# Other places for a batch's products in an attention and MLP block of eight batches, and doubled products without reader in batches 0 and 1

## The reference

```python
mod = (_silu(c) @ wmod).reshape(8, 6, 1, 128)            # sa, ca, ga, sb, cb, gb
h = _layernorm(x) * (1 + ca) + sa
q, k, v = split(h @ w_qkv.T)                             # 16 heads of 8
s = q @ k.T * 8 ** -0.5
s = s - max(s)
p = where(s >= 0, 1 + s*(1 + s/2*(1 + s/3)), 1 / (1 - s*(1 - s/2*(1 - s/3))))
x = x + ga * ((p / sum(p)) @ v @ w_out.T + b_out)
h = _layernorm(x) * (1 + cb) + sb
h = s0 * concat(h, -h) @ W0; h = relu(h) * 2
h = s1 * h @ W1;             h = relu(h) * 2
x = x + gb * (s2 * h @ W2)
```

## Time and profile before

| | |
|---|---|
| median of 3 runs | 709.76 us |
| the profiled execution's own time | 708.76 us |
| its span, first to last instruction | 706.9 us |
| TensorE (PE) busy | 627.4 us, 3019 products |
| VectorE (DVE) busy | 646.2 us |
| ScalarE (ACT) busy | 598.8 us |
| GpSimd (POOL) busy | 599.0 us |
| mean granted TensorE clock | 0.97 of full |

### The profile page before, as it was taken

How to read it: one execution, slowest core, us unless ns; L and a number is a source line. 1 busy time by engine, 2 the same in 40 slices (tenths; PEclk the granted TensorE clock), 3 DMA queues, 4 the chain that set the end, 5 groups by cost and what they waited for, 6 DMA issues and landing times.

```text
span 706.9 us, 9679 instructions
## 1 busy us (share of the span) xinstructions
PE 627.4 (89%) x3019; PEld 244.5 (35%) x3019; DVE 646.2 (91%) x768; ACT 598.8 (85%) x606; POOL 599.0 (85%) x390
## 2 busy tenths in 40 slices
PE   7577787877789999899989999899989999997798
PEld 5222222223222344233423333233423343334266
DVE  6899988989999999999999999999999999998943
ACT  2647877978899999999999989999999989998932
POOL 7769777897989999899989999899989989798920
PEclk9579999999999999999999999999999999999999
DMA  7514112141124222141224122241125112101001
GB/s 206 160 46 165 48 51 61 54 149 32 55 58 144 81 58 73 48 159 32 57 76 168 50 58 75 60 167 41 40 61 172 53 54 72 54 10 27 17 12 30
DMA packets 37783, 53.61 MB, mean 76 GB/s; under 512 B 11308, under 2 KB 20804, under 8 KB 37732
## 3 DMA queue, kind: packets, MB, share of 16 engines
q1 hardware_dynamic: 36766, 51.81, 24.1%
q10 hardware_dynamic: 966, 1.19, 0.6%
HBM read 29.17 MB, written 18.36 MB: 67 GB/s over the span
## 4 chain that ended last, share of the span: by engine, by line
PE 56%; DVE 17%; ACT 12%; issue 11%; POOL 2%; SPq 1%; DMA 1%; ACTq 0%; DVEq 0%; POOLq 0%
PE MB L515 13%; PE OP L593 12%; PE Z L561 9%; PE SA L576 8%; DVE cub L966 8%; DVE mx L975 7%; ACT sq L720 5%; ACT prob L734 4%; PE MB L528 3%; PE MB L505 2%; PE MB L612 2%; PE MB L486 1%; PE OP L443 1%; DVE st L1012 1%; PE MB L493 1%
## 5 line engine op out<-in xcount | busy, mean ns | idle before, releaser
L1201 POOL TENSOR_TENSOR cub<-cub 128x2048 f32<-128x2048 f32 x127 | 456.8, 3602 | 48.4 <-DVE cub L966 48.1
L720 ACT ACTIVATE sq<-Z,shift 128x1024 f32<-128x1024 f32 x256 | 282.3, 1116 | 58.5 <-PE Z L561 56.8
L966 DVE SCALAR_TENSOR_TENSOR cub<-sq,Z 128x1024 f32<-128x1024 f32 x256 | 309.8, 1211 | 13.0 <-ACT sq L720 12.2
L975 DVE TENSOR_REDUCE mx<-SA 128x2 f32<-128x1024 f32 x248 | 301.9, 1217 | 15.6 <-PE SA L576 12.2
L734 ACT ACTIVATE prob<-cub 128x2048 f32<-128x2048 f32 x128 | 244.3, 1910 | 0.4 <-PE OP L593 0.4
L576 PE MATMUL SA<-KH,QL 64*128 64x512 f32 x496 | 121.1, 485 | 33.4 <-DVE mx L975 29.3
L561 PE MATMUL Z<-QH,KH 64*128 64x512 f32 x512 | 128.8, 499 | 17.7 <-DVE cub L966 16.5
L593 PE MATMUL OP<-prob,Vq 128*16 128x512 f32 x1024 | 136.6, 607 | 0.0
L561 PEld LDWEIGHTS Z<-QH,KH 64*128 64x128 f32 x512 | 48.4, 185 | 197.6 <-DVE cub L966 121.6
L515 PE MATMUL MB<-hid,W 128*128 128x512 f32 x192 | 108.0, 645 | 0.0
L576 PEld LDWEIGHTS SA<-KH,QL 64*128 64x128 f32 x496 | 47.4, 187 | 111.1 <-DVE mx L975 89.4
(11 more groups left out here) (205 smaller groups left out, 501.6 us busy)
## 6 DMA issues: line engine op xcount, KB each, us to landing
QL<-parts_q SPq DMA_DIRECT2D x62, 128.0 KB, 2.6
KH<-parts_k SPq DMA_DIRECT2D x62, 128.0 KB, 2.7
QH<-parts_q SPq DMA_DIRECT2D x62, 128.0 KB, 2.7
parts_q<-SQ SPq DMA_DIRECT2D x28, 256.0 KB, 2.5
parts_k<-SK SPq DMA_DIRECT2D x28, 256.0 KB, 2.7
QH<-mp SPq DMA_DIRECT2D x253, 2.0 KB
nd<-OT SPq DMA_DIRECT2D x124, 32.0 KB
out<-y SPq DMA_DIRECT2D x7, 256.0 KB, 2.8
```

What stands on the lines that cost most here:

```text
L720: nc.scalar.activation(sq[:, h, :], Z[:, h, :], ACT.Square, bias=shift[:, 0:1]).then_inc(s_sq, 1)
L966: nc.vector.scalar_tensor_tensor(cub[:, m % RING, h, :], sq[:, h, :], CUB_ADD, Z[:, h, :], ALU.add, ALU.mult).then_inc(s_cv, 1)
L975: nc.vector.tensor_reduce(to, unit_bank(m, u)[:, :, :], AX_X, ALU.max).then_inc(s_mx, 1)
L1201: nc.gpsimd.tensor_tensor(ff, ff, ff, ALU.mult).then_inc(s_fp, 1)
```

## The change

It gives new places to all products of batches 0 to 6 in `MAIN`, to l0 in batch 7, and to l1_3 of batch 6; it issues two products instead of one at each place of `FILL`, and takes other places for it; it moves xbg and wog; it turns the order of SyncE's queue in a step; it moves batch 6's x1n from VectorE to GpSimd, and changes the order behind the last step.

```diff
 MAIN = [
-    ("hT", 1, [(0, "c", 4)]), ("q", 1, [(0, "d", 4)]), ("k", 1, [(1, "d", 4)]),
-    ("l1_0", -2, [(2, "c", 1), (2, "d", 1), (3, "c", 1), (3, "d", 1)]),
-    ("l1_1", -2, [(4, "c", 1), (4, "d", 1), (5, "c", 1), (5, "d", 1)]),
-    ("l1_2", -2, [(6, "c", 1), (6, "d", 1), (7, "c", 1), (7, "d", 1)]),
+    ("l1_0", -2, [(0, "c", 1), (0, "d", 1), (1, "c", 1), (1, "d", 1)]),
+    ("hT", 1, [(2, "c", 4)]), ("q", 1, [(2, "d", 4)]), ("k", 1, [(3, "c", 4)]),
+    ("l1_1", -2, [(3, "d", 1), (4, "c", 1), (4, "d", 1), (5, "c", 1)]),
+    ("l1_2", -2, [(5, "d", 1), (6, "c", 1), (6, "d", 1), (7, "c", 1)]),
+    ("v", 1, [(7, "d", 4)]),
     ("x1", -1, [(8, "c", 2), (8, "d", 2)]),
     ("l1_3", -2, [(9, "c", 1), (9, "d", 1), (10, "c", 1), (10, "d", 1)]),
-    ("v", 1, [(11, "c", 4)]),
-    ("y", -2, [(11, "d", 1), (12, "c", 1), (12, "d", 1), (13, "c", 1)]), ("h2T", -1, [(13, "d", 4)]),
+    ("y", -2, [(11, "c", 1), (11, "d", 1), (12, "c", 1), (12, "d", 1)]), ("h2T", -1, [(13, "d", 4)]),
...
-    ("l0_0", -1, [(11, "c", 4)]), ("l0_1", -1, [(12, "c", 4)]), ("l0_2", -1, [(13, "c", 4)]), ("l0_3", -1, [(14, "c", 4)]),
+    ("l0_0", -1, [(12, "b", 4)]), ("l0_1", -1, [(13, "b", 4)]), ("l0_2", -1, [(14, "b", 4)]), ("l0_3", -1, [(15, "b", 4)]),
...
-    ("l1_2", -2, [(2, "c", 4)]), ("l1_3", -2, [(4, "b", 2), (4, "c", 2)]), ("y", -2, [(5, "c", 3), (5, "d", 1)]),
+    ("l1_3", -2, [(0, "b", 3), (0, "c", 1)]), ("l1_2", -2, [(2, "c", 4)]), ("y", -2, [(5, "c", 3), (5, "d", 1)]),
...
-FILL |= {(0, n): ("k", 2) for n in range(2, 12)} | {(0, n): ("v", 2) for n in range(12, 16)}
-FILL |= {(1, n): ("k", 3) for n in range(2, 8)} | {(1, n): ("x1", 1) for n in range(9, 12)} | {(1, 12): ("v", 3)}
+FILL = {(FIRST, n): ("v", 1) for n in range(13, 16)} | {(0, n): ("v", 1) for n in range(3)}
+FILL |= {(0, n): ("k", 2) for n in range(4, 8)} | {(0, n): ("v", 2) for n in range(8, 16)}
+FILL |= {(1, n): ("v", 2) for n in range(3)} | {(1, n): ("k", 3) for n in range(4, 8)}
+FILL |= {(1, n): ("x1", 1) for n in range(9, 14)}
...
-MAIN_AT = {"xbg": 6, "wog": 5, "den_sq": 6, "den_inv": 6, "att": 7, "st2": 9, "mv2": 10, "rs2": 11, "x1n": 11,
+MAIN_AT = {"xbg": 1, "wog": 2, "den_sq": 6, "den_inv": 6, "att": 7, "st2": 9, "mv2": 10, "rs2": 11, "x1n": 11,
...
-AT[B] = MAIN_AT | {"w2g": 0, "wog": 1, "xbg": 1}
+AT[B] = MAIN_AT | {"xbg": 0, "wog": 0, "w2g": 1}
...
-                    product(B, "l1_3", B - 2): (SA[:, 0, :], product(B - 1, "l1_0", B - 2)),
+                    product(B, "l1_3", B - 2): (Z[:, 1, 0:S], None),
...
                     pe.wait_ge(s_wts, 1)
-                    nc.tensor.matmul(MB[:, :], ident[:, :], W1f[:, n % KC, :], start=True, stop=True)
+                    for kc in (n % KC, (n + 1) % KC):
+                        nc.tensor.matmul(MB[:, :], ident[:, :], W1f[:, kc, :], start=True, stop=True)
```

107 lines of the change are left out of this document (50 added, 57 removed).

## The result

The changed kernel took 722.74 us in the median of 4 runs (722.69 to 723.08); the kernel before, run beside it, 709.23 (706.82 to 710.2). The ratio is 1.019, 95% interval 1.017 to 1.021: slower by 13.5 us, where a time of 715, some 5 us slower, was forecast; 722.74 lies above the range of 711 to 719 and the wider one of 708 to 721. The profiled execution took 722.73 us, with a span of 720.9 against 706.9.

The account below looks back on a forecast made before the run. VectorE's work sets the floor, 4.54 us a step; in batches 0 and 1 the SA loop, 4.62, is just over it. Terms 0.4 - 0.9 + 4.0 + 4.2 - 1.0 - 1.3 = +5.4 gave 714.2, as median 715, range 711 to 719.

Parts of the forecast that it names:

- The start: Steps ahead of batch 0, where three places are doubled too: +0.4 us, bounds 0 and 2.6.
- Batch 0, steps 0 to 4: No `with_v` yet, so VectorE's floor holds; with hT, q and k some 0.9 more: 24.0 against 24.9 us, -0.9.
- Batch 0, steps 5 to 15: Eleven doubled places in the loop between SA products, 5.48 each, 0.2 for v: 60.5 against 56.5 us, +4.0.
- Batch 1: Twelve doubled places, 65.8 us, with hT, k, x1 and statistics priced by step: 86.0 against 81.8, +4.2.
- The clock: TensorE's clock taken as full from batch 0 on; by the skill's idle rule three falls would stay, 5 us more.
- Batches 2 to 6: Moved products: -1.6 from ScalarE's full stretch, +1.1 from four late steps, +0.3 KH wait: -0.2 us a batch.
- Batch 7 to step 15: x1n leaving VectorE gives -2.3, l0 at place b costs +3.5: step 15 starts 1.1 us later.
- Behind it: Behind batch 7's last steps, l1_3 fills PE's wait and identity products precede the pick: -2.4 of 42.2 us.
- A: Rival: the second product is free in batches 0 and 1, about 4.7 us a step, total about 699; chance 0.08.
- B: Rival: the clock stays low over the start of batch 0, +5 us, total 720; chance 0.12.
- C: Rival: the middle gives all it can, -1.5 us a batch in batches 2 to 6, total about 708.7; chance 0.12.
- D: Rival: the KH read is late behind the writes, 1 us more in five batches, +5, total 720; chance 0.13.

Follow-up runs that it names:

- e2: The changed kernel with l0 of batch 7 put back at place c of steps 11 to 14; 719.40 us.
- e3: The changed kernel with the second product without reader moved behind the second SA product of its step, in 22 of 27 places; 711.72 us.
- e5: The changed kernel with product v back in step 11 at place c, and y a half step later; 726.62 us.
- e6: The changed kernel with l0 of batch 7 at its old places and x1n of batch 6 on VectorE again; 722.53 us.
- e1_single: The changed kernel with one product without reader, not two, at each place of FILL; 716.30 us.
- e4_before_doubled: The kernel before with two products at each of its own places of FILL, nothing else changed; 721.95 us.
- e17_x1n_gpsimd: The same kernel as e16, with batch 6's x1n on GpSimd; 693.96 us.
- e14: The kernel before with the new end, products without reader at place d (none in step 11), new places for l1_0, hT, q, k, and early writes of parts; 694.93 us.
- e16: The same kernel as e14, with the products without reader doubled ahead of batch 0 and in its steps 0 to 2; 694.69 us.
- e11_sp_order: The kernel before with SyncE's order of the change alone; 716.51 us.
- e8_end_fill_at_d: The kernel before with the change's order behind the last step and single products without reader at place d, except in step 11; 697.78 us.

## Why the prediction was wrong

The sign held, and so did the mechanism of the loop; the sum was +5.4 and the measured one +14.0 in the profiled executions. The missing 8.6 lie in three terms, batch 7 (3.6 short), batches 2 to 6 (3.1) and batch 1 (2.1); the others nearly cancel. By its steps:

- **The start, +0.4.** Measured -0.3. Of the five kernels with the changed start the others (e2, e3, e5, e6) begin batch 0 at 40.7 to 41.4, so this says little.
- **Batch 0, steps 0 to 4, -0.9.** Measured -0.3. hT, q and k in steps 2 and 3 cost 1.3 and not 0.9 (step 3 took 5.87), and step 0 took 4.84, not 4.54.
- **Batch 0, steps 5 to 15, 60.5.** Measured 60.2, and right by luck, through two errors that cancel. The loop with the pair is 5.38, not 5.48, which over eleven steps is 1.1 less. And I missed a wait that the change adds: the pair of step 8 waits for ScalarE to take v from 7d, 1.44, where I had priced v's new place at 0.2; steps 8 and 9 took 1.5 more than in e5_v_at_11. I had looked at who waits behind v's copy on ScalarE and not at the product that writes v's bank next.
- **Batch 1, 86.0.** Measured 88.1. Step 3 took 6.54, not 5.1: hT stands in the loop with 0.66, and q's wait for its copy, 0.96, behind SA and ahead of Z, is paid too. Steps 14 and 15 took 10.35, not 9.7, with `cub` waiting 0.90 behind h2T's copy. Step 7 took 6.56 and not 5.5: ScalarE's two `den` instructions, 0.62 and 0.63, stand ahead of `prob` and of the square for the next `cub`, which waited 1.40 for it. I had counted them in the middle and not here; the shorter loop hides it, for the twelve doubled steps together took 66.6, as forecast. The product for q, and the `cub` that opens step 8:

```profile
144.28 1.10 PE L486 MATMUL MB<-hT,wq 128*128 128x512 f32 x2 [0.96 <-ACT hT L750]
...
170.01 1.22 DVE L971 SCALAR_TENSOR_TENSOR cub<-sq,Z 128x1024 f32<-128x1024 f32 x1 [1.40 <-ACT sq L725]
```

- **The clock.** Right for batches 0 to 6. The Trainium skill (TensorE: Matmul & The Clock Gate, "What's actually happening") ties a fall to an idle window; by that rule as I had read it the fall at 92.9 would have stayed. The measurement decides: in the kernel before the clock fell at 92.9, 113.4 and 154.3 although TensorE was never idle for over 0.92 us at a time in the 10 us ahead, and with the doubled products these falls are gone; with the second product left out (e1_single) batches 0 and 1 have five again. It isn't a safe rule: e4_before_doubled and e5_v_at_11, doubled as well, had falls of 13.7 and 3.4 us and of 6.8 us there. For batch 7 I was wrong, having read no clock at all: 6.8 us at 0.50, next to idle times of 2.64 and 1.92.
- **Batches 2 to 6, -0.2 each.** Measured +0.4 each, which is 3.1 us short in five. In the changed kernel's batch 5 the waits of VectorE are (what waits, for what: us in total, times, longest)

```profile
DVE mx L980 <- PE SA L579: 1.6, 6, 0.4
DVE cub L971 <- ACT sq L725: 0.5, 3, 0.2
```

and on TensorE, of those that ScalarE ends,

```profile
PE MB L486 <- ACT hT L750: 1.0, 1, 1.0
PE MB L489 <- ACT hid L780: 0.6, 1, 0.6
...
PE MB L518 <- ACT SK L759: 0.3, 1, 0.3
```

  The gain from the clogged stretch of the earlier trace rows was 1.1 (0.53 in step 1, 0.57 in steps 13 and 14), where I had 1.6. What came back was 0.9 through the half step behind k, that is l1_1 and l1_2 copied at "c", and 0.5 for v in steps 8 and 9: 1.4 and not 1.1. I had priced four steps at ScalarE's 0.27 each and given the half step no price of its own. The KH wait of 0.3 wasn't there: the read landed 1.1 us before its SA product.
- **Batch 7 to step 15, +1.1.** Measured +4.7, the worst term. x1n on GpSimd is worth 0.9, not 2.3 (steps 10 and 11 took 9.71 against 10.63; e17_x1n_gpsimd has the same). I had put the 1.65 of idle before the `cub` of step 12 down to the Z product behind l0_0, and let it go with l0_0. It is still 1.65 with l0_0 gone from there, in the row at 663.21 above, as it is with l0_0 at 11c in e17_x1n_gpsimd: ScalarE has `prob` (until 661.50) and the copy of h2T ahead of the squares, as in the kernel before.

```profile
661.41 0.77 ACT L774 ACTIVATE h2T<-MB,mod 128x512 f32<-128x512 f32 x1
662.07 2.12 ACT L725 ACTIVATE sq<-Z,shift 128x1024 f32<-128x1024 f32 x2
```

  l0 at place b takes 5.18 a step as I had said, where the clock is full (step 14); steps 12 and 13, with a fall each, took 6.45 and 6.13, 2.2 more. Why the clock falls there stays open.
- **Behind it, -2.4.** Measured -2.3, right; 1.1 of it by the new order alone.

Of the rivals, A (the second product free) is out: its work costs at least 7.5 in two batches. B was out of place: the clock fell in batch 7, not in batch 0. C didn't come: the middle took 0.4 more a batch and not 1.5 less; the best middle of any kernel here (e14, e16) is 0.45 less. D was real and not in this kernel: in e11_sp_order the late reads cost 1.1 to 1.4 a batch, more than my 1.0, though not through writes and reads in one row as I had it; the changed kernel escapes them because TensorE's loads of instructions happen to lie elsewhere.

## What to carry to other kernels

A product that is there only to hold TensorE's clock belongs where the dependency loop has slack, and it must write a bank that nobody is waiting to have copied; moving it by half a step was worth 8 us (705.5 to 697.8), doubling it where it stood cost 14 (707.9 to 722.0), and leaving it out cost 14 against the best place (694.5 to 708.4). When an edit changes a stretch that it doesn't touch, look for what moves with the length of the code before giving the edit a price. Read the clock in every stretch that a forecast changes, not only in those where it is low now.

## What the runs showed of the hardware

- Loads of instructions take part in the traffic. With one packet of 16 KB among eight writes of 256 KB, single writes landed after 4.1 to 4.5 us instead of 2.5 to 2.9 and the KH reads behind them were issued 1.1 to 1.6 us later, and it recurs in each batch. In the changed kernel's trace 25 packets of 16 KB on queue 8 and 27 of 8 KB on queue 14 run within the span. The Trainium skill (Runtime: NRT & Kernel Launch, "Instruction fetch mechanics") has an engine's sequencer bring in the next block of 16 KiB over a DMA queue of its own while it executes, at a cost that is mostly hidden. The packets of queue 8 agree with the size; in e11_sp_order the cost isn't hidden, with waits of 1.1 to 1.4 us a batch.
- Whether the clock falls in a stretch isn't settled by the products in it. TensorE's products of batch 7 are the same in the kernel before, e8_end_fill_at_d and e11_sp_order, and the profiled executions have no fall there, one of 3.4 us and one of 10.2 us.
- Without products to hold it, the granted clock in batches 0 and 1 was 0.74 and 0.83 in the mean, and the runs of that kernel spread over 10 us, those of e17_x1n_gpsimd over 0.4.
